# Sorting edges into bins: ranks from one-hots and pair comparisons in place of a scan

## The reference

```python
edge_index = jnp.stack([src, dst])
x = _layernorm(x + _L0_gnn_ref(x, src, dst, edge_weight, w_self, w_neigh), axis=-1)
x = _layernorm(x + _L1_gnn_ref(x, edge_index, W1, b1, W2, b2, eps, gamma, beta), axis=-1)
x = _layernorm(x + _L2_gnn_ref(x, W_gc, ..., beta, src, dst), axis=-1)
x = _layernorm(x + _L3_gnn_ref(x, src, dst, edge_weight, weight, learnable_diag, bias), axis=-1)
```

```python
# L0: msgs = edge_w[:, None] * x[src]; sum over dst; out = x @ w_self.T + sums @ w_neigh.T; out / |out|
# L1, three times: agg = segment_sum(h[src], dst)
#     h = relu(layer_norm(relu(((1 + eps) * h + agg) @ W1 + b1) @ W2 + b2 + h))
# L2: m = segment_sum((x * rsqrt(deg_out))[src], dst) * rsqrt(deg_in)
#     x = m @ W_gc + b_gc + x @ W_res + b_res; then a top-2 mixture of 64 experts and a batch norm
# L3: e1 = segment_sum(w[:, None] * x[col], row); (x - e1 * (diag + 1)) @ weight + bias
```

## Time and profile before

| | us |
|---|---|
| median of 3 runs | 5051.05 (5048.02 to 5051.4) |
| profiled execution, its own time | 5044.36 |
| its span | 5042.7 |

### The profile page before, as it was taken

How to read it: one execution, slowest core, us unless ns; L and a number is a source line. 1 busy time by engine, 2 the same in 40 slices (tenths; PEclk the granted TensorE clock), 3 DMA queues, 4 the chain that set the end, 5 groups by cost and what they waited for, 6 DMA issues and landing times.

```text
span 5042.7 us, 84235 instructions
## 1 busy us (share of the span) xinstructions
PE 4521.2 (90%) x25611; PEld 3799.3 (75%) x25611; DVE 3787.4 (75%) x12117; ACT 2599.1 (52%) x6315; POOL 3296.0 (65%) x3281
## 2 busy tenths in 40 slices
PE   6888888879998899989989699995999878999997
PEld 4777777679997688867777588874999745888885
DVE  7889888559998699859988565667999666555553
ACT  4888888636643445535555344431555423444442
POOL 6767676767777666667666577771455455777776
PEclk9999999999998999989999799997999978999998
DMA  6444444488889888898878988884686533343343
GB/s 169 132 131 126 125 134 126 151 287 273 267 264 307 268 250 252 255 324 267 259 242 250 319 264 257 259 242 141 221 265 206 179 89 113 112 114 113 114 114 97
DMA packets 547534, 1018.20 MB, mean 202 GB/s; under 512 B 104874, under 2 KB 320168, under 8 KB 546796
## 3 DMA queue, kind: packets, MB, share of 16 engines
q0 software_dynamic: 210144, 646.68, 42.8%
q1 hardware_dynamic: 319658, 350.32, 21.3%
q10 hardware_dynamic: 17280, 15.74, 0.9%
HBM read 896.63 MB, written 117.06 MB: 201 GB/s over the span
## 4 chain that ended last, share of the span: by engine, by line
PE 46%; DVE 7%; POOL 5%; issue 5%; DMA 4%; ACT 0%; SPq 0%; ACTq 0%; DVEq 0%; POOLq 0%
PE PS L2578 14%; PE PS L2646 4%; PE PS L2816 4%; PE PS L2825 4%; PE PS L2549 4%; PE PS L2556 4%; PE PS L2711 3%; POOL ring L2474 2%; PE PS L2603 2%; PE PS L2696 1%; POOL ring L2503 1%; DMA ring<-expert_outputs,ring 1%; PE PS L2685 1%; PE PS L2834 1%; DVE slot_picks L3197 1%
## 5 line engine op out<-in xcount | busy, mean ns | idle before, releaser
L2474 POOL DMA_INDIRECT slot_rows<-planes,REC x1656 | 1611.9, 973 | 684.2 <-issue 444.5
L3039 ACT ACTIVATE wide_blocks<-HH 128x512 fp32r<-128x512 uint8 (+1 forms) x1456 | 823.0, 575 | 824.1 <-PE PS L2578 664.2
L2578 PE MATMUL PS<-plane_rows,wide_blocks 128*128 128x512 f32 x3920 | 1030.2, 410 | 22.0 <-ACT wide_blocks L3039 20.2
L2578 PEld LDWEIGHTS PS<-plane_rows,wide_blocks 128*128 128x128 f32 x3920 | 732.2, 192 | 178.1 <-ACT wide_blocks L3039 23.3
L2474 POOL DMA_INDIRECT ring<-in_x,REC x555 | 545.1, 982 | 217.4 <-issue 151.2
L2556 PE MATMUL PS<-ring,pick 128*128 128x256 f32 x2082 | 570.1, 408 | 69.0 <-DMA ring<-in_x,REC 34.2
L2474 POOL DMA_INDIRECT ring<-table,REC x486 | 465.3, 957 | 225.7 <-issue 216.2
L2556 PEld LDWEIGHTS PS<-ring,pick 128*128 128x128 f32 x2082 | 398.3, 201 | 170.2 <-DMA ring<-in_x,REC 46.2
L3004 ACT ACTIVATE HH<-iota,HH 128x128 bf16<-128x128 f32 (+1 forms) x1040 | 355.9, 391 | 267.3 <-PE PS L2603 255.7
L2646 PE MATMUL PS<-HH 128*128 128x256 f32 x2058 | 489.4, 379 | 0.0
L2494 POOL DMA_INDIRECT ring<-second_outputs,ring x120 | 237.9, 1983 | 326.7 <-PE PS L2806 238.4
(11 more groups left out here) (383 smaller groups left out, 8955.6 us busy)
## 6 DMA issues: line engine op xcount, KB each, us to landing
HH<-dense_blocks SPq DMA_DIRECT2D x728, 112.0 KB
HH<-in_L_gnn_w SPq DMA_DIRECT2D x128, 512.0 KB, 5.5
plane_rows<-planes SPq DMA_DIRECT2D x64, 768.0 KB, 8.4
planes<-HN SPq DMA_DIRECT2D x188, 256.0 KB, 4.5
slot_rows<-planes,REC POOLq DMA_INDIRECT x1656
dense_blocks<-HH SPq DMA_DIRECT2D x24, 784.0 KB
expert_outputs<-ring ACTq DMA_DIRECT2D x120, 128.0 KB, 4.0
ring<-in_x,REC POOLq DMA_INDIRECT x555
```

The source lines that it names most:

```text
L2474: pool.indirect_dma_start(to, None, planes[k] if dense else tables[k], bass.IndirectOffsetOnAxis(ap=at_rows, axis=0)).then_inc(s_slot[slot ...
L2578: last = mm(bank(5 + n % 2, RP), WIDE[:, at_block:at_block + P], plane(0, t, RP), start=t == 0, stop=t == NT - 1)
L3039: fn(WIDE[:, e % XA * XW:e % XA * XW + w], AB[n % QA][:, lo:lo + w], ACT.Copy).then_inc(s_ax, 1)
```

## The change

All of it is in `sort_into_bins` and its scratch, on VectorE. PE's, ScalarE's, POOL's and SP's streams keep their instructions and their order. VectorE's has 10448 rows in place of 10773.

The rank of an edge is now a sum of two things. `AHEAD`: the one-hots of the edge times PE's counts of the lanes before, which picks the count of its own source tile. `SAME`: for every pair of edges in a lane whether their source tiles are equal, times `UPTO`, a mask of ones for the pairs (k, j) with j up to k. Both lie side by side in `RANKS`, and one reduction over 49 + 18 elements gives the rank. The one-hots are stored with the edge outside and the source tile inside (`OHS1`), so that the sum over the lane's edges reads with a stride of 49 words. The fields go to PSUM at once (`FLDP`), their bfloat16 parts cut off by a mask of the upper 16 bits; the weight's three parts are added by one reduction; BADV is gone, its count now comes from the bins kept.

```diff
-        OHCU = scratch(2 * NT * (WT + 1))
-        OHB = OHCU[:, 0:NT * (WT + 1)].rearrange("p (s k) -> p s k", s=NT)
-        CUB = OHCU[:, NT * (WT + 1):].rearrange("p (s k) -> p s k", s=NT)
+        OHCU = scratch(OHW)
+        OHS1 = OHCU[:, 0:WT * NT].rearrange("p (k s) -> p k s", k=WT)
...
+        RANKS = MVFR[:, 0:WT * (NT + WT)].rearrange("p (k s) -> p k s", k=WT)
+        AHEAD, SAME = RANKS[:, :, 0:NT], RANKS[:, :, NT:NT + WT]
+        UPTO = scratch(WT * WT).rearrange("p (k j) -> p k j", k=WT)
...
                 if n == 0:
                     if b == 0:
                         dve.wait_ge(s_frow, 96)
+                        V.link(v.memset(UPTO, 0.0))
+                        for c in range(WT):
+                            v.memset(UPTO[:, c, 0:c + 1], 1.0)
...
-                    v.memset(NONE, 0.0)
...
-                    v.tensor_copy(FLDB[:, 2, :], at_weight)
+                    v.tensor_scalar(FLDP[:, 2, :].bitcast(i32), R[:, t, 2, :], top, None, ALU.bitwise_and)
...
-                    v.tensor_copy(FLDB[:, 3, :], rest_)
+                    v.tensor_scalar(FLDP[:, 3, :].bitcast(i32), rest_.bitcast(i32), top, None, ALU.bitwise_and)
+                    v.scalar_tensor_tensor(base, code, 1.0, own, ALU.add, ALU.mult)
                     V.link(v.scalar_tensor_tensor(s1, code, 1.0, own, ALU.add, ALU.mult))
...
-                    V.link(v.tensor_tensor(ohs, iota[:, 1:NT + 1].unsqueeze(2).broadcast_to((P, NT, WT)),
-                                           s1.unsqueeze(1).broadcast_to((P, NT, WT)), ALU.is_equal))
-                    v.scalar_tensor_tensor(most, most, BIN + 0.5, own, ALU.add, ALU.mult)
-                    v.tensor_reduce(BCNT, ohs, AX.X, ALU.add).then_inc(s_bd, 1)
+                    v.tensor_tensor(SAME, base.unsqueeze(2).broadcast_to((P, WT, WT)), s1.unsqueeze(1).broadcast_to((P, WT, WT)), ALU.is_equal)
+                    V.link(v.tensor_tensor(OHS1, iota[:, 1:NT + 1].unsqueeze(1).broadcast_to((P, WT, NT)),
+                                           s1.unsqueeze(2).broadcast_to((P, WT, NT)), ALU.is_equal))
+                    v.tensor_reduce(BCNT, OHS1.rearrange("p k s -> p s k"), AX.X, ALU.add).then_inc(s_bd, 1)
                 if n == 4:
+                    v.tensor_tensor(SAME, SAME, UPTO, ALU.mult)
                     dve.wait_ge(s_bp, 2 * b + 1)
-                    V.link(v.tensor_tensor(BSUM, bank(7, NT), BCNT, ALU.add))
-                    v.tensor_copy(OHB[:, 0:1, 0:1], bank(7, 1).unsqueeze(2))
-                    V.link(v.tensor_tensor(OHB[:, 1:NT, 0:1], bank(7, NT - 1, 1).unsqueeze(2), BSUM[:, 0:NT - 1].unsqueeze(2), ALU.subtract))
-                    flat = OHB.rearrange("p s k -> p (s k)")
-                    V.link(v.tensor_tensor_scan(CUB.rearrange("p s k -> p (s k)"), flat, NONE.broadcast_to((P, NT * (WT + 1))), 0.0, ALU.add, ALU.max))
-                    V.link(v.tensor_tensor(RANKS.rearrange("p k s -> p s k"), cus, ohs, ALU.mult))
+                    V.link(v.tensor_tensor(AHEAD, OHS1, bank(7, NT).unsqueeze(1).broadcast_to((P, WT, NT)), ALU.mult))
                 if n == 5:
...
-                    V.link(v.tensor_tensor(valid, rank, most, ALU.is_lt))
+                    V.link(v.scalar_tensor_tensor(valid, rank, -(BIN + 0.5), most, ALU.add, ALU.is_lt))
...
-                    v.tensor_tensor(BADV[:, :], BADV[:, :], valid, ALU.add)
...
                 if n == 7:
-                    v.tensor_copy(FLDP, FLDB)
...
-                    V.link(v.tensor_copy(bins[:, 3, :], moved(2)))
-                    V.link(v.tensor_tensor(bins[:, 3, :], bins[:, 3, :], moved(3), ALU.add))
-                    V.link(v.tensor_tensor(bins[:, 3, :], bins[:, 3, :], moved(4), ALU.add))
+                    v.tensor_reduce(bins[:, 3, :], bank(7, 3 * BC, 64 + 2 * BC).rearrange("p (f c) -> p c f", f=3), AX.X, ALU.add)
...
-                        v.tensor_reduce(col[:, 11:12], BADV[:, :], AX.X, ALU.add)
...
-                        v.tensor_reduce(HELD5, OWN5.rearrange("p (s c) -> p s c", s=NT), AX.X, ALU.add).then_inc(s_bad, 1)
+                        V.link(v.tensor_reduce(HELD5, OWN5.rearrange("p (s c) -> p s c", s=NT), AX.X, ALU.add))
+                        v.tensor_reduce(col[:, 11:12], HELD5, AX.X, ALU.add).then_inc(s_bad, 1)
```

More of the change, by code:

```diff
@@ L1607, in gnn @@
         FLAG = sb("FLAG", 1, i32)
-        BADV = sb("BADV", WT)
         STI = sb("STI", NT, i32)
@@ L3218, in sort_into_bins @@
                     v.tensor_scalar(lane, at_source, P - 1, None, ALU.bitwise_and)
[L3219 removed]
+                    v.tensor_scalar(FLDP[:, 2, :].bitcast(i32), R[:, t, 2, :], top, None, ALU.bitwise_and)
                     V.link(v.tensor_scalar(own, dl, 0.0, None, ALU.is_ge))
[L3221 to L3223 removed]
+                    v.tensor_scalar(FLDP[:, 0, :], dl, 1.0, None, ALU.add)
@@ L3224, in sort_into_bins @@
+                    v.tensor_scalar(FLDP[:, 1, :], lane, 1.0, None, ALU.add)
+                    v.tensor_tensor(rest_, at_weight, FLDP[:, 2, :], ALU.subtract)
                     V.link(v.scalar_tensor_tensor(own, dl, float(P), own, ALU.is_lt, ALU.mult))
-                    v.tensor_copy(FLDB[:, 3, :], rest_)
+                    v.tensor_scalar(FLDP[:, 3, :].bitcast(i32), rest_.bitcast(i32), top, None, ALU.bitwise_and)
+                    v.scalar_tensor_tensor(base, code, 1.0, own, ALU.add, ALU.mult)
@@ L3226, in sort_into_bins @@
                     V.link(v.scalar_tensor_tensor(s1, code, 1.0, own, ALU.add, ALU.mult))
-                    v.tensor_tensor(FLDB[:, 4, :], rest_, FLDB[:, 3, :], ALU.subtract)
+                    v.tensor_tensor(FLDP[:, 4, :], rest_, FLDP[:, 3, :], ALU.subtract)
                     v.tensor_scalar(most, s1, float(t + 1), 64.0 * (2 * BC - NT) - 1.0, ALU.is_equal, ALU.mult)
-                    V.link(v.tensor_tensor(ohs, iota[:, 1:NT + 1].unsqueeze(2).broadcast_to((P, NT, WT)),
-                                           s1.unsqueeze(1).broadcast_to((P, NT, WT)), ALU.is_equal))
@@ L3635, in block_constants @@
                 V.link(v.memset(UP[0:BIN, 1:2], float(P)))
-            v.memset(BADV[:, :], 0.0)
             v.memset(LEAST[:, :], LN_EPS)
```

17 lines of the change are left out of this document (6 added, 11 removed).

## The result

The changed kernel takes 4994.8 us (median of 4 runs, 4988.9 to 4997.71) against 5049.53 us (median of 4, 5047.45 to 5051.4) for the kernel before. The ratio is 0.9886, 95% interval 0.9872 to 0.9899: 55 us faster. The forecast was 4997 us.

The account below looks back on a forecast made before the run. Pass 0 was taken as bound by POOL's pitch, PE and waits in turn, pass 1 by POOL alone. Gains 26 + 7.5 + 7 + 13.5 = 54 us took 5051.05 to 4997 us; bounds 4985 to 5010, range 4967 to 5038.

Parts of the forecast that it names:

- Step 4: In sort_into_bins on VectorE: 4.43 us replaced by two products, together 1.52 us, saving 2.91 us a bin.
- Step 5: In sort_into_bins: reduction grows from 882 to 1206 elements, sum into BADV goes; net +0.25 us a bin.
- Step 10: In sort_into_bins: three linked operations, 0.65 us, become one reduction of 78 elements, about 0.15; saves 0.5 us a bin.
- Step 0: In sort_into_bins: comparison of pairs and small operations +0.33 us, reduction now reading with a stride +0.7 us a bin.
- Pass 0, waits of PE: Pass 0: PE's waits for VectorE shrink; L2685 18.6 us, L2593 9, L2589 -2; sum 26 us.
- POOL held by L3240: Passes 0 and 1: gathers no longer stretched beside the strided product L3240; 7 us in pass 0, 7.5 in pass 1.
- Pass 1: POOL alone sets the pace, a faster VectorE gives nothing except through POOL; 7.5 us gained, mean gather 965 ns.
- Pass 3: Between 2311.8 and 2772.0 us, ten PE waits at L2685 shorten or go: 17.6 us, of which 13.5 kept.
- rival 2: Second periods of pass 0 and pass 3: shorter waits keep PE's clock up, another 10 to 25 us go, about 4975; chance 0.14.
- rival 1: Waits come back elsewhere, at ScalarE or PE's own work; only POOL's 14.5 us stays, 5036 us; chance 0.20.
- second period: Pass 0, second of each three of nine steps (27 gathers): 38.7 us, bound by waits; seven long ones shorten by 18.6 us.
- rival 4: Hold on POOL stays because any large VectorE product causes it: 40 us gained, 5011; chance 0.60 together with the forecast.

Follow-up runs that it names:

- pad_step4: Changed kernel with three more linked products behind step 4, 3.0 us more VectorE a bin, one input in PSUM: 5065.24 us, ratio 1.0023.
- counts_from_sbuf: Changed kernel with the counts copied from PSUM to SBUF and the large product taking both inputs from SBUF: 5006.56 us, ratio 0.9909.
- counts_copied: Changed kernel with the counts also copied to SBUF, but the large product still reading them from PSUM: 4996.42 us, ratio 0.9889.
- straight_write: Kernel before with RANKS stored the other way round, so L3240 writes straight and L3242 reads with a stride: 5047.66 us, ratio 0.9986.

## Why the prediction was right, point by point

**The cost on VectorE was right, term by term.** Step 4: 1.50 us measured, 1.52 forecast. Step 5: +0.24 against +0.25. Step 7, from the first of its two products to the work behind them: 3.17 us where it took 3.33 with the cast, -0.16 as forecast. Step 10: -0.50 as forecast. Step 0 with the reduction: 4.79 us from its start at 421.79 to the next work at 426.58, against 3.88 before (399.94 to 403.82), +0.91 against 0.33 + 0.7 = 1.03. Together 2.93 - 0.24 - 0.91 + 0.16 + 0.50 = 2.44 us a bin against 2.3; these are the steps of one bin of pass 0. Each came from a row of before with the same number of elements; the one that had no such row, the strided read, was priced by the nearest strided write at 1741 ns and came at 1715. The Trainium skill's rule that each access to a new 16-byte line pays a penalty ("SBUF — State Buffer", "Door 1: The DMA port swizzle") spoke for the same choice, and the trace agrees: 1715 ns against 1065.

**Pass 0, waits of PE: sum near, terms not.** Pass 0 as a whole was to lose 33 us, 26 of them here and 7 by POOL, and lost 27.0. PE's idle time, in which POOL's part is contained, fell from 1010.2 - 865.45 = 144.8 to 983.2 - 862.13 = 121.1, 23.7 us. L2685: 37.2 to 21.8, 15.4 us of 18.6, since each of the seven long waits lost 2.1 to 2.4 us, not 2.66. The forecast let VectorE be 2.66 us earlier at L3502, as if all else arrived when it did before; that PE now arrives earlier too would make the difference, but this was not isolated. pad_step4, with 3.0 us more on VectorE there, has the same seven waits at 5.0 to 5.6 us, 3 us above the changed kernel's. L2593: 13.6 to 11.4. This step failed: I let 9 us of short waits go. They went at their old places and others came, at 413.47 with 1.95 us and at 523.94 with 2.64. Where a wait ends PE's delay at one place, PE comes sooner to the next operand of VectorE's; a wait that is shorter than what VectorE saves is not thereby gone. L2589: forecast to grow by 2, it fell by 1.6, though VectorE's step 0 is longer. ScalarE's L2965 had no term and gave 7.7 us (24.2 to 16.5). PE's waits for gathers at L2556 grew by 1.4 + 4.0 us, which is where POOL became the last. Of the signs named ahead, "waits at L2685 halved in passes 0 and 3" did not come: they fell from 37.2 to 21.8 us and from 35.4 to 33.1.

**POOL held by L3240.** Cause right (counts_from_sbuf against counts_copied), size not confirmed. In pass 0 it was put at 7 us. There the hold's end is worth 3.0 us with the new steps, which is within the spread of single executions, and its shortening with the old steps nothing (1010.2 to 1011.3). In pass 1 it was put at 7.5; the shortening gives 0.5 with the old steps, the end of the hold 6.6 with the new ones. It was given a sum of its own, as if it did not matter how late VectorE is.

**Pass 1.** 9.9 us against 7.5, and the mean gather 963 ns against 965. The sentence that POOL alone sets the pace there and a faster VectorE gives nothing is false: pad_step4 lengthened that pass by 13.6 us with VectorE's time alone. Shorter steps with the hold in place took it from 579.6 to 577.0 us. In straight_write 6 us of shorter gathers brought 0.5 us while the old steps stood; that the 6.6 us of the hold's end would have stayed away with them too is likely but was not run. The forecast of this pass was near by luck: VectorE's part was put at nothing, and POOL's was counted as if it came out in full by itself.

**Pass 3.** 20.3 us against 13.5. In its middle PE's idle time fell from 460.2 - 422.07 = 38.1 to 439.9 - 413.16 = 26.7, 11.4 us, where I had kept 13.5. The waits for VectorE, before and after in the middle:

```profile
PE PS L2685 <- DVE TZ L3471: 22.2, 12, 4.9
```
```profile
PE PS L2685 <- DVE TZ L3466: 16.4, 10, 4.1
```

They gave 5.8 us, not 17.6: again short waits did not vanish but stood elsewhere. Other waits on the list (for ScalarE at L2711, L2696 and L2578, together 15.0 before and 10.1 after) gave 4.9. The other 8.9 us are PE's busy time, with 13 fewer matmuls in the records, which is at most some 3 us. The rest, some 6 us, has about the size of what the clock gave: the granted clock of the middle rose from 0.97 to 0.98, by the two digits some 4.5 us of 450. The same stretch of the other kernels has the same order: 0.97 in 459.0 us (straight_write), 0.98 in 443.3 (counts_copied), 0.98 in 440.0 (counts_from_sbuf), 0.96 in 466.5 (pad_step4). This is a part of rival 2, which the forecast kept out of its sum. It was not isolated by a run of its own.

**Two readings of the prediction were wrong.** In rival 1 ScalarE is said to be at 33 to 37 us in each of the three periods; the earlier trace rows have it at 36.65, 29.47 and 33.00, so in the second period, where the long waits were looked for, it had more room than was said. And rival 4's 5011 lies just outside the forecast's own 4985 to 5010, though inside the whole range. Neither moves the sum.

**What was not seen.** The gain of pass 0 was to come from the second periods, as the long waits at L2685 stand there, and from short waits in the first ones, which are bound by PE. To compare like with like, a period is marked here by PE's own matmuls on the 27 rows that the gathers of the earlier trace rows fetch; PE works on them 3 to 19 us after POOL, and all seven long waits lie in second periods by these marks too. From the fourth period to the twenty-fourth, the seven second periods lost 1.0 to 2.7 us each (32.4 to 30.8 for the one with the wait at 418.56), 12 us in all. The third periods lost 12 us as well (44.8 to 41.4 in the best case, 40.5 to 40.4 in the worst). The first ones, for which 9 us had been counted, stayed at 38.4 and 40.5 us in turn. Marked by the gathers themselves it looks otherwise: the first of the earlier trace rows went from 42.6 to 37.7 us, the second from 38.7 to 37.8. So the gain came half where it was looked for and half in a place to which the forecast gave nothing but a loss.
